# Causal attention stage: row-maxima DMA ahead of the stores, two heads per set of stores, key scores two steps later

## The reference, cut to what matters

```python
def _L1_attn_ref(x, Wk, Wq, Wv, Wp, bp):
    B, T, C = x.shape                      # 32, 1024, 96
    H = N_HEADS                            # 6
    hs = C // H                            # 16
    k = (x @ Wk).reshape(B, H, T, hs)
    q = (x @ Wq).reshape(B, H, T, hs)
    v = (x @ Wv).reshape(B, H, T, hs)
    wei = jnp.einsum('bhtd,bhsd->bhts', q, k) * C ** (-0.5)
    wei = jnp.where(mask, wei, -jnp.inf)   # mask: lower triangle
    wei = jax.nn.softmax(wei, axis=-1)
    out = jnp.einsum('bhts,bhsd->bhtd', wei, v).reshape(B, T, C)
    return out @ Wp + bp
```

## Time and profile before

| what | value |
|---|---|
| median of 3 runs | 2862.11 us (2858.29 to 2863.71) |
| the profiled execution, its own time | 2865.3 us |
| its span, first to last instruction | 2863.6 us |
| mean granted TensorE clock | 0.972 of 2.4 GHz |
| attention stage, first to last row maxima | 1002.9 us to 2372.7 us of the span |
| busy over the whole span | PE 89%, DVE 75%, ACT 68%, POOL 42% |

### The profile page before, as it was taken

The page is one execution under the profiler, slowest core; times in us unless marked ns, Lnnn a source line. Parts: engine busy times, 40 slices in busy tenths (PEclk is TensorE's granted clock), DMA queues, the critical chain, the costliest instruction groups (busy, mean ns, idle before and its releaser), DMA issues. The chain is left out here.

```text
span 2863.6 us, 84442 instructions
## 1 busy us (share of the span) xinstructions
PE 2557.5 (89%) x29309; PEld 1513.6 (53%) x29309; DVE 2146.2 (75%) x3217; ACT 1952.5 (68%) x3751; POOL 1200.3 (42%) x2352
## 2 busy tenths in 40 slices
PE   4999999999999598888888888898888887899996
PEld 2555555555555255555555555555555554455553
DVE  3576666667675287888888888888888884678987
ACT  2677777777777356666666666676666674577775
POOL 0133333323333344555555555555555552224445
PEclk9999999999999779999999999999999998999998
DMA  1123222322222365555555556555555563334555
GB/s 35 45 67 100 66 99 66 99 76 89 92 84 78 95 105 106 111 112 111 110 113 110 112 112 110 111 111 111 111 111 110 111 116 101 100 101 130 144 143 155
DMA packets 785166, 290.88 MB, mean 102 GB/s; under 512 B 710545, under 2 KB 768178, under 8 KB 785074
## 3 DMA queue, kind: packets, MB, share of 16 engines
q1 hardware_dynamic: 783730, 288.46, 44.1%
q10 hardware_dynamic: 1344, 1.18, 0.1%
HBM read 100.77 MB, written 87.29 MB: 66 GB/s over the span
## 5 line engine op out<-in xcount | busy, mean ns | idle before, releaser
L1028 DVE TENSOR_REDUCE at_row_max<-at_ps_queries 128x1 f32<-128x1024 f32 (+7 forms) x1536 | 1071.6, 749 | 208.5 <-PE at_ps_queries L909 208.2
L982 ACT ACTIVATE at_probs<-at_ps_keys 128x512 f32<-128x512 f32 x1344 | 744.3, 598 | 175.8 <-PE at_ps_keys L924 175.6
L924 PE MATMUL at_ps_keys<-at_turned 50*128 50x128 f16 (+3 forms) x3456 | 579.8, 276 | 140.2 <-DMA at_turned<-at_max_rows 128.8
L899 PE MATMUL at_ps_queries<-at_turned 48*128 48x512 f16 (+3 forms) x2304 | 614.8, 335 | 55.4 <-DVE at_row_max L1028 25.8
L944 PE MATMUL at_ps_values<-at_probs,at_v 128*32 128x128 f32 x10752 | 418.4, 281 | 0.4 <-DVE at_out L1018 0.4
L924 PEld LDWEIGHTS at_ps_keys<-at_turned 50*128 50x128 f16 x3456 | 223.7, 94 | 348.4 <-ACT at_probs L982 190.2
L982 ACT ACTIVATE at_diag_probs<-at_ps_keys 128x512 f32<-128x512 f32 x384 | 208.4, 595 | 252.4 <-PE at_ps_keys L924 252.3
L944 PEld LDWEIGHTS at_ps_values<-at_probs,at_v 128*32 128x32 f32 x10752 | 261.7, 110 | 98.4 <-issue 75.6
L841 POOL TENSOR_TENSOR at_max_parts<-at_row_max,at_max_unit 128x8 f16<-128x8 f32 x192 | 38.8, 202 | 635.0 <-DVE at_row_max L1028 635.0
L907 PE MATMUL at_ps_queries<-mask_queries,shifted 64*128 64x256 bf16 (+1 forms) x960 | 244.0, 254 | 0.0
L513 POOL TENSOR_TENSOR cb_o_hat<-cb_o,cb_o_scale 128x768 f32<-128x768 f32 x32 | 48.0, 1501 | 461.6 <-DVE cb_o_scale L433 461.6
(11 more groups left out here) (222 smaller groups left out, 5012.6 us busy)
## 6 DMA issues: line engine op xcount, KB each, us to landing
qkv_rows<-cb_packed SPq DMA_DIRECT2D x32, 1152.0 KB, 7.6
at_stacks<-qkv_rows SPq DMA_DIRECT2D x192, 192.0 KB, 2.9
cb_x<-in_x_dram SPq DMA_DIRECT2D x32, 384.0 KB, 3.6
cb_x_again<-in_x_dram SPq DMA_DIRECT2D x32, 384.0 KB, 4.5
x_after_conv<-cb_x SPq DMA_DIRECT2D x32, 384.0 KB, 5.0
attention_rows<-at_att SPq DMA_DIRECT2D x768, 8.0 KB, 1.4
ff_att_rows<-attention_rows SPq DMA_DIRECT2D x32, 384.0 KB, 4.4
ff_x<-x_after_conv SPq DMA_DIRECT2D x128, 96.0 KB, 2.3
```

The costliest lines, as they stand in the source:

```text
L899: mm = pe.matmul(scores[:, c0:c0 + width], QT[Q_ROWS, slot, qb * P:(qb + 1) * P], KT[Q_ROWS, slot, k0 * P:k1 * P], start=(c0 == 0), stop=True,
L924: mm = pe.matmul(pk[:, bank_k, c0:c0 + n * P], KT[K_ROWS, slot, kb * P:(kb + 1) * P], QT[K_ROWS, slot, q0 * P:(q0 + n) * P], start=(c0 == ...
L982: act.activation(probs, pk[:, ring(r, u + (u > MAX_TURN)), :], ACT.Exp, scale=scale).then_inc(S["probs"], 1)
L1028: ins = dve.tensor_reduce(MX[:, r % 2, qb:qb + 1], pq[:, (NR * r + g) % QBUFS, b0 * P:(b0 + n) * P], AX.X, ALU.max)
```

## The change

Three edits, all in `causal_attention`:

1. SP's `body` issues the row maxima of head i - 3 (L817 before, L808 now) before the stores instead of after them.
2. The stores are done for two heads at a time, in every second iteration (r even), as five DMAs of 64 KB and four times 16 KB in place of ten of half that size. A row of the store is now partition x 2 heads x 64 numbers; the runs of 64 numbers (256 bytes) are as before. The head of the pair that is ready first waits one iteration longer. There are three `stored` semaphores in place of six; the AT slots are six as before, and POOL still waits for stores of six heads earlier.
3. LAG is 13 in place of 11: unit k = 0 of the key scores of head h is at step 4 of iteration h + 4, unit 8 at step 3 of iteration h + 5. The steps of the query scores, the turning of the maxima (step 5) and the values (steps 1, 4, 7) stay.

```diff
-    LAG = 11
+    LAG = 13
...
-    STORES = 1 + SPAN
+    PAIR, STORES = 2, 1 + SPAN
...
-        stored = [sem(f"stored{i}") for i in range(SLOTS)]
+        stored = [sem(f"stored{i}") for i in range(SLOTS // PAIR)]
...
-        dst = att.rearrange("b l (j d) -> (b l j) d", d=HD).rearrange("(h a q p c) d -> h a q p (c d)", a=2, q=SPAN,
-                                                                       p=VW, c=SPAN)
+        dst = att.rearrange("b l (j d) -> b (l j) d", d=HD).rearrange(
+            "b (x h a q p c) d -> b x a q p h (c d)", x=HEADS // PAIR, h=PAIR, a=2, q=SPAN, p=VW)
...
-                    if on(7):
-                        q = (r - 7) % SLOTS
-                        sp.wait_ge(S["out_ready"], i - 6)
-                        halves = AT[:, q, :, :].rearrange("p (a c) d -> p a (c d)", a=2)
-                        sp.dma_start(dst[i - 7][0].rearrange("q p n -> (q p) n"), halves[:, 0, :]
-                                     ).then_inc(stored[q], 16)
-                        for n in range(SPAN):
-                            sp.dma_start(dst[i - 7][1][SPAN - 1 - n], halves[n * VW:(n + 1) * VW, 1, :]
-                                         ).then_inc(stored[q], 16)
                     if on(3):
                         q = (r - 3) % SLOTS
                         sp.wait_ge(S["max_copied"], i - 2)
                         sp.dma_start(QT[MAX_ROWS, q, :], MT[:, q % 2, :]).then_inc(max_in[q], 16)
+                    if on(7) and r % PAIR == 0:
+                        q, b = (r - 8) % SLOTS, lap + (r - 8) // SLOTS
+                        sp.wait_ge(S["out_ready"], i - 6)
+                        pair = AT[:, q:q + PAIR, :, :].rearrange("p h (a c) d -> p a h (c d)", a=2)
+                        sp.dma_start(dst[b][q // PAIR][0].rearrange("q p h n -> (q p) h n"), pair[:, 0, :, :]
+                                     ).then_inc(stored[q // PAIR], 16)
+                        for n in range(SPAN):
+                            sp.dma_start(dst[b][q // PAIR][1][SPAN - 1 - n], pair[n * VW:(n + 1) * VW, 1, :, :]
+                                         ).then_inc(stored[q // PAIR], 16)
...
-                        _above(pool.wait_ge, stored[q], STORES * _dmas(lap, r, 6 + SLOTS, SLOTS))
+                        _above(pool.wait_ge, stored[q // PAIR], STORES * _dmas(lap, r, 6 + SLOTS, SLOTS))
```

More of the change, by code:

```diff
@@ L817, in body @@
                         sp.dma_start(QT[MAX_ROWS, q, :], MT[:, q % 2, :]).then_inc(max_in[q], 16)
+                    if on(7) and r % PAIR == 0:
[7 more added lines that the diff above has]
+                                         ).then_inc(stored[q // PAIR], 16)
                 _pipeline(sp, body, NHEADS, 8, SLOTS, ahead=1)
-                for r in range(SLOTS):
-                    sp.wait_ge(stored[r], STORES * 16 * (NHEADS // SLOTS))
+                for n in range(SLOTS // PAIR):
+                    sp.wait_ge(stored[n], STORES * 16 * (NHEADS // SLOTS))
             @block.gpsimd
```

## The result

The changed kernel takes 2780.97 us (median of 4 runs, 2777.58 to 2782.0) against 2862.59 us before (median of 4, 2858.29 to 2863.71): ratio 0.9716, 95% interval 0.9699 to 0.9732. It is faster by 82 us, and lies 8 us above the 2773 of the prediction, inside its range.

The account below looks back on a forecast made before the run. SP's DMA issuing was taken as the bound. 174 heads x (7.15 - 6.65) = 87, plus 2 at the ends, gave 89 us off 2865.3; with 3.2 us to the median, 2773 us, range 2745 to 2812.

Parts of the forecast that it names:

- The bound: Attention loop: SP's issuing of DMAs sets the period, at 7.1 to 7.3 us per head; no compute engine is full.
- Rival E: SP's rows show pushing back by the 16 DMA engines, so pairing stores frees nothing: 2862 us; chance 0.03.
- D: Transposes land later behind doubled store bytes, 5.4 instead of 4.6 us: 2825 us, half the effect 2800; chance 0.13.
- C: The two-step shift also removes part of DVE's 0.4 us idle time, 6.35 us per head: 2721 us; chance 0.06.
- F: Issues cost by piece or byte, so each paired store takes twice as long, 7.8 us per head: 2975 us; chance 0.04.
- The floor of PE and DVE: Attention loop: PE and DVE together need 6.56 us per head when SP has a lead.
- rival B: The two-head chain does not bind; PE and DVE alone set 6.50 to 6.60 us per head: 2757 us; chance 0.24.
- The chain over two heads: Transpose, query scores, turned maxima, copy, maxima DMA, stores, load, next transpose: 13.4 us summed, 13.2 taken, for two heads.
- Key scores two steps later: PE asks for the maxima about 1.5 us later in the loop; this buys slack and no time: zero.
- The new order: Maxima DMA ahead of stores lands two us early, ending PE's wait; stores, load and transpose then queue behind SP's wait.
- the clock: TensorE's clock falling to half for about two us, more or fewer times in a denser loop: a few us either way.
- A: The likeliest case: the two-head chain nearly meets the PE and DVE limit, 6.6 to 6.75 us per head: 2773 us; chance 0.50.

## Why the prediction came out right, point by point

**The bound.** Right. SP was full of DMA issues: taking half the store issues away, and nothing else, gave 2756.8 us, and neither the order alone nor the steps alone gave anything (2867 and 2869 us). Rival E (pushing back by the DMA engines) is out by the same run, D (longer landing) by the landings, 4.6 us at the median before and after, C by the gaps, none of them under 6.54 us in the loop, and F (cost by the piece) by the paired issues: 0.41 us for the store of 256 pieces, 0.33 for 64 (0.39 and 0.32 before). I had added 0.1 us per pair for this, and it is 0.02 + 4 x 0.01 = 0.06.

**The floor of PE and DVE.** 6.56 us from three heads with SP ahead; measured 6.57 in every second head of the changed kernel and in nearly every head with paired stores alone. The number given for rival B, 2757 us, is the time of that version. The prediction had reached that time from another side too: if issue time is no bound, the early maxima bring all of it and the merging nothing. It was the other way round, since the early maxima alone gave nothing and the merging alone gave 105 us. The Trainium skill, page "DMA: Bandwidth & Descriptors", section "Issuing engines are not separate DMA queues", calls the time to initiate a DMA usually small beside the DMA. The trace does not agree for the transposes here, whose issue takes 2.9 of the 4.6 us to their landing, and SP's issues filled the 7.15 us of a head.

**The chain over two heads.** Right in its parts: I had summed 13.4 and allowed 13.2 for the late start of PE; measured 13.13 where PE waits, with 4.82 for landing and start, 4.30 for the middle step (4.6 less the 0.2 to 0.3 expected), 0.03 for SP's release (0.1 was taken) and 3.98 for SP's part. Over the loop its mean is 13.24, so 13.2 was nearer than 13.4. Every second head stands at 6.57, and the chain sets the one between. Without the three falls of the clock the loop's mean is (1159.7 - 12.2) / 173 = 6.63, where 6.65 was taken.

**Key scores two steps later.** Zero, right: 2780.97 and 2780.68 us with 13 and 11. I had called it slack; one pair of experiments, in which the maxima go out 1.5 us later, shows slack that is used (24 us).

**The new order.** Here the prediction had said "the wait of PE ends by this alone, as long as SP keeps up", and had gone on to price the chain that it closes. It had not drawn the conclusion, that with pairs the wait ends without the new order too, and that the new order then only costs. That cost is 24 us with LAG 11 and 19 with LAG 13. This is no error of the sum but a part of the working that was left out: I summed the three edits together and never one against the other two.

**The size.** 8 us under the measured time, and so close partly by luck, since two errors offset each other. The loop took 6.70 us per head where 6.65 was forecast: 9 us too little. The written-out iterations gained 6.7 us where 2 were taken: nearly 5 too much. The last 3 to 4 us are the correction from the profiled execution to the median, 3.2 us before and none after (2780.74 and 2780.97). The term that was mis-sized in the loop is the clock, "a few us either way": the three gaps at its start cost 12 us. They do not look like chance. They come in the changed kernel and again with LAG 11, three times each, always on a transpose that lands 5.7 to 6.3 us after its issue. Such late landings are in the kernel with paired stores alone too (6.1 us for the transpose at 1076, 6.0 for the one at 1094), but there the chain has slack, and no gap of DVE in its loop is over 7.1 us. Why transposes land late at the start of the stage stays open; they already did so in the kernel before. Of the 24 us between this kernel and paired stores alone, the loop's period has (6.703 - 6.575) x 173 = 22, of which the three gaps are 12 and the heads of 6.6 to 6.9 us the rest. Not tried: shortening the chain by issuing the load behind the transpose.

**The range.** 2745 to 2812 held the time. **The signs to look for** were there: the wait for the maxima gone, one for transposes of some tenths in every second head, DVE busy 0.915 of the stretch, idle time on SP before the maxima of every second iteration. One sign of being wrong was there by its letter as well: a new wait of PE of more than 0.1 us per head. The wait for the transposes is 50.4 us over 174 heads, 0.29 each, of which 7.8 us are in the three gaps; but it is the wait that the prediction had itself named for A.

## What to carry to other kernels

A queue that only issues DMAs shows no busy share, so look at its timeline when no engine is full: if its rows and gaps add up to the period, fewer issues are the cure, and moving one issue ahead of another only moves the stall. Once the queue has slack, put DMAs that nobody waits for into the time in which it would wait anyway, ahead of the wait and not behind it: the same five stores cost 19 to 24 us on the way from one semaphore to the next transpose, and nothing beside it. When several edits go in together, price each with and without the others; here one of three carried more than the whole gain.

## What the runs showed of the hardware

- The cost of an issue on SP did not follow size: 0.33 us for 32 partitions of the paired store, 0.41 for 128, but 0.69 for 64. Cutting the first store in two took 1.55 us for its issues in place of 0.41, and 1.46 us more from the maxima to the next transpose, not the 0.5 that I had taken.
- In the changed kernel's loop each of three waits of PE of 2.2 to 3.2 us was followed by a stretch with a granted clock of 0.50 to 0.52 (1.2 of 2.4 GHz); waits of 0.7 us were not. In the kernel with the cut store PE waited 1.8 us at the median in every pair, and the clock fell in 40 of 86: the length of the wait alone does not tell. A pair with a fall took 1.8 us longer there (16.23 against 14.46).
- Each group of values (f32) between scores (f16) costs PE 0.14 us beyond its matmuls, whatever the size of the group; at the step to the key scores the weight load stands 0.20 us, 1142 times of 1142 with seven groups per head and 532 of 532 with three.
